# A mixture-of-experts layer on one core: the first chunk's router weights are turned, applied as a bias and split in another order

## What is computed

```
xn = layernorm(x)
x  = x + graph(xn, edges) + attention_and_mlp(xn)
f  = layernorm(x)
w  = softmax(f @ Wr + br)                     # router, 8 weights a row
h  = relu(bn1(f @ W1[e] + b1[e]))             # for each expert e
h  = relu(bn2(h @ W2[e] + b2[e]))
x  = x + sum_e w[:, e] * (h @ Wo[e] + bo[e])
```

## Time and profile before

| | |
|---|---|
| device time, median of 3 runs | 1095.93 us (1095.89 to 1095.94) |
| profiled execution, device time | 1095.72 us |
| its span | 1093.9 us |
| PE busy | 1082.8 us, 99% of the span |
| DVE busy | 768.1 us, 70% |
| ACT busy | 732.0 us, 67% |
| POOL busy | 248.3 us, 23% |
| mean granted TensorE clock | 0.998 |
| chunk 0's expert rounds | about 176 to 219 us of the span |

### The profile page before, as it was taken

How to read it: one execution, slowest core, us unless ns; L and a number is a source line. 1 busy time by engine, 2 the same in 40 slices (tenths; PEclk the granted TensorE clock), 3 DMA queues, 4 the chain that set the end, 5 groups by cost and what they waited for, 6 DMA issues and landing times.

```text
span 1093.9 us, 19080 instructions
## 1 busy us (share of the span) xinstructions
PE 1082.8 (99%) x6512; PEld 967.6 (88%) x6512; DVE 768.1 (70%) x1804; ACT 732.0 (67%) x1275; POOL 248.3 (23%) x290
## 2 busy tenths in 40 slices
PE   9999998999999999999999999999999999999998
PEld 7988987988888888888898888888888988889998
DVE  8888756886686676766766767767767667676665
ACT  5777756676675666756756767667567566576665
POOL 4787763312012012030120120210301202100000
PEclk9999999999999999999999999999999999999999
DMA  6878852111011101110110111101101101100000
GB/s 182 270 226 252 243 171 54 60 34 55 1 49 50 40 18 42 40 58 2 44 55 1 49 50 39 47 13 40 59 1 49 50 10 35 35 20 1 1 20 15
DMA packets 71300, 67.91 MB, mean 62 GB/s; under 512 B 20641, under 2 KB 66579, under 8 KB 71203
## 3 DMA queue, kind: packets, MB, share of 16 engines
q1 hardware_dynamic: 66552, 59.34, 18.1%
q0 software_dynamic: 3968, 6.71, 2.4%
q10 hardware_dynamic: 683, 0.64, 0.2%
HBM read 40.87 MB, written 25.80 MB: 61 GB/s over the span
## 4 chain that ended last, share of the span: by engine, by line
PE 91%; POOL 3%; DVE 2%; issue 2%; ACT 1%; DVEq 0%; POOLq 0%; ACTq 0%
PE bank L280 29%; PE bank L281 29%; PE bank L282 29%; PE bank L989 1%; POOL gathered L601 1%; PE bank L1156 1%; PE bank L1164 1%; PE bank L930 1%; PE bank L1179 1%; PE bank L922 1%; POOL gathered L619 0%; POOL alpha_l L621 0%; PE bank L946 0%; DVE sum_squares L1336 0%; DVE activated L1260 0%
## 5 line engine op out<-in xcount | busy, mean ns | idle before, releaser
L1380 DVE SCALAR_TENSOR_TENSOR accumulated<-bank,router_w,accumulated 128x256 f32<-128x256 f32 (+2 forms) x392 | 170.4, 480 | 177.9 <-PE bank L282 171.0
L665 ACT ACTIVATE h<-weight_stage 128x512 fp32r<-128x512 f32 (+2 forms) x206 | 113.6, 599 | 183.9 <-PE bank L282 164.4
L282 PE MATMUL bank<-ffn_w_high,h 128*128 128x256 f32 (+2 forms) x778 | 220.0, 283 | 0.0
L281 PE MATMUL bank<-ffn_w_low,h 128*128 128x256 f32 (+2 forms) x778 | 219.8, 283 | 0.0
L280 PE MATMUL bank<-ffn_w_high,h 128*128 128x256 f32 (+2 forms) x778 | 219.6, 282 | 0.0
L1230 DVE TENSOR_TENSOR h_low<-activated,h_high 128x512 fp32r<-128x512 f32 (+2 forms) x208 | 135.3, 658 | 76.0 <-ACT h_high L665 73.0
L816 ACT ACTIVATE activated<-bank,bn_cols 128x512 f32<-128x512 f32 (+2 forms) x208 | 155.8, 749 | 46.1 <-PE bank L282 44.1
L816 ACT ACTIVATE weight_stage<-bank,bn_cols 128x512 f32<-128x512 f32 (+2 forms) x208 | 152.7, 748 | 41.4 <-PE bank L282 41.0
L280 PE MATMUL bank<-xT_high,ffn_w_high 128*128 128x512 f32 (+2 forms) x416 | 158.9, 382 | 0.1
L280 PE MATMUL bank<-h_high,ffn_w_high 128*128 128x512 f32 (+2 forms) x416 | 157.9, 380 | 0.1
L281 PE MATMUL bank<-xT_low,ffn_w_high 128*128 128x512 f32 (+2 forms) x416 | 157.8, 379 | 0.0
(11 more groups left out here) (228 smaller groups left out, 1917.1 us busy)
## 6 DMA issues: line engine op xcount, KB each, us to landing
x_rows<-in_x SPq DMA_DIRECT2D x18, 512.0 KB, 4.8
x_turned<-xT_high SPq DMA_DIRECT2D x22, 256.0 KB, 3.6
x_turned<-xT_low SPq DMA_DIRECT2D x22, 256.0 KB, 4.7
out<-accumulated SPq DMA_DIRECT2D x11, 512.0 KB, 3.3
mix_xT_high<-x_turned SPq DMA_DIRECT2D x10, 512.0 KB
mix_xT_low<-x_turned SPq DMA_DIRECT2D x10, 512.0 KB
weight_stage<-in_L_ffn_W SPq DMA_DIRECT2D x16, 256.0 KB, 3.2
node_table<-gathered SPq DMA_DIRECT2D x22, 132.0 KB, 2.9
```

Of the source, the lines that this page charges most:

```text
L281: nc.tensor.matmul(dst, ah, bl, start=False, stop=False)
L282: last = nc.tensor.matmul(dst, al, bh, start=False, stop=(k == n - 1))
L665: return nc.scalar.activation(dst, src, ACT.Copy)
L1380: last = V.scalar_tensor_tensor(a, y_of(ch, e)[b][0:tp, (t % 2) * D:(t % 2 + 1) * D], wts(ch)[0:tp, t, e:e + 1], a, ALU.mult, ALU.add)
```

## The change

All of it concerns chunk 0. PE turns the router weights behind `L2` of round 1 in place of round 0, and multiplies them with `bo` behind `L2` of round 2 in place of round 1. ACT copies the turned weights at the end of `relu2(1)` in place of `relu2(0)`. DVE does `hid1(1)` ahead of `weights` in place of behind them, does `add_bias` in round 2, behind `hid1(3)`, in place of round 1, and `accumulate(0)` no longer waits for `add_bias`; `accumulate(1)` and later do. No instruction with work in it is added or removed; only order and waits are changed.

```diff
@@ ACT
                     relu2(ch, e)
-                    if e == 0 and ch.c == 0:
+                    if e == 1 and ch.c == 0:
                         router_turned(ch)
@@ PE
                     L2(ch, e)
                     if ch.c == 0:
-                        if e == 0:
+                        if e == 1:
                             router_turn(ch)
-                        elif e == 1:
+                        elif e == 2:
                             out_bias(ch)
@@ DVE, accumulate
-                need(dve, s["fai"], ch.b0 + ch.nb)
+                need(dve, s["fai"], ch.b0 + ch.nb if ch.c > 0 else min(e, 1))
@@ DVE, add_bias
                     need(dve, s["fbo"], ch.b0 + b + 1)
+                    if ch.c == 0:
+                        need(dve, s["acc"], 1)
@@ DVE, ahead of the loop and in it
             hid1(CHUNKS[0], 0)
             route(CHUNKS[0])
+            hid1(CHUNKS[0], 1)
             weights(CHUNKS[0])
...
-                    if e + 1 < NE:
+                    if ch.c == 0 and e == 0:
+                        pass
+                    elif e + 1 < NE:
                         hid1(ch, e + 1)
...
-                    if e == 1 and ch.c == 0:
+                    if e == 2 and ch.c == 0:
                         add_bias(ch)
                     if e > 0:
                         accumulate(ch, e - 1)
```

## The result

| | before | changed |
|---|---|---|
| median, beside each other (13 runs each) | 1095.88 us | 1098.41 us |
| ratio, 95% interval | | 1.0025 [1.0017, 1.0034] |
| span of the profiled execution | 1093.9 us | 1096.3 us |

The account below looks back on a forecast made before the run. PE, busy 99% of the span, was taken as the bound. The profiled 1095.72 + 1.63 (later `mix2`) + 1.6 (clock) = 1098.95; for the median, 1095.93 + 3.2 = 1099.1 us, range 1097.1 to 1099.9.

Parts of the forecast that it names:

- first two cases: `mix2`'s new wait with a slow stretch behind it, 1099.1 +- 0.4, chance 0.65; wait alone, 1097.6 +- 0.3, chance 0.21.
- signs of being wrong: `logits` starting before 187.0, DVE's chain from 188.8 to 194.5 being shorter, or the clock staying at 1.00.
- The change at its own place: Chunk 0: `L1(2)` starts at 181.62, held by ACT; moving `hid1(1)` brings nothing; `router_turn` waits for nothing; PE 2.4 us ahead.
- The first place where the gain goes: DVE's `logits` of chunk 1 stays at 187.35; `L2(2)` waits 1.1 us for `hid1(2)`; PE's lead shrinks to 0.93 us.
- The second place: `mix2` of chunk 1 waits 2.5 us for the later `add_bias` and starts at 194.56.
- 1.63 us later than before: `mix2` of chunk 1 starts at 194.56 in place of 192.93.
- the old place costs 1.6 + 1.6 us: At `router_turn`, chunk 0: wait 1.6 us plus slow stretch 1.6 us, 3.2 us, the most the change could bring.
- The clock, 1.6 us: Behind `mix2`'s new wait: a stretch at clock 0.50, priced between 0 and 1.6 us, taken as 1.6.
- The lower bound: Clock price of 0: a wait of 1.5 us ahead of 174.50 left the clock at 1.00.
- the second case: `mix2`'s new wait alone, with the clock left at full: 1097.6 +- 0.3 us, chance 0.21.

Follow-up runs that it names:

- weights_first: The changed kernel with `weights` ahead of `hid1(1)` on DVE again, as before: 1098.08 us beside 1095.73, ratio 1.0025.
- bias_late_alone: The kernel before with only `add_bias` of chunk 0 moved to round 2 behind `hid1(3)`, with its waits: 1099.85 us, ratio 1.0033.
- exp_behind: The changed kernel with `add_bias` ahead of `weigh`, `hid1(2)` ahead of `logits`, and `router_exp` behind `relu1(1)`: 1092.25 us beside 1095.54, ratio 0.9973.
- after_look: The changed kernel itself, profiled a second time; no timed ratio; from the first transposition, `mix2` starts at 20.88 us and the span ends at 923.4.

## Why the prediction was right, and where it was off

The direction was right, and 1098.41 lies in the range, 0.7 us below the predicted 1099.1. The mechanism, `mix2` waiting for a late `add_bias`, was right too. But the time was hit partly by luck: it lies between the prediction's first two cases (1098.7 to 1099.5 and 1097.3 to 1097.9) and in neither. One of its own signs of being wrong, a clock that stays at 1.00, came in the first profile.

- *The change at its own place*: right. `L1(2)` waits 0.84 us for ACT, `router_turn` for nothing, and in the first profile the slow stretch is gone. Moving `hid1(1)` brought nothing (weights_first).
- *The first place where the gain goes*: right. `logits` stays, at 12.9 for 13.0, and `L2(2)` waits: `L1(3)` started at 187.26, took 1.35, and `L2(2)` started at 189.61, so 1.0 us from start to start (1.1 forecast); the profile shows 0.84, since the last matmul's modelled end lies behind its slot.
- *The second place*: right to 0.1 us. 194.56 - 174.32 = 20.24 was forecast, 20.18 measured (PE started 0.15 us behind `add_bias`, not 0.05), and bias_late_alone shows that this part alone does it.
- *The term "1.63 us later than before"*: mis-sized. It was taken against a profile of before with a slow stretch. Against one without it, it is 20.18 - 17.90 = 2.3 us, and the ends agree: 921.1 - 918.8 = 2.3. Behind this is the sentence that the old place costs 1.6 + 1.6 us, the most that the change could bring. The slow stretch costs 0.7 there and not 1.6, because `logits` holds DVE and DVE holds PE. I had found this limit for the changed kernel and hadn't asked it of the kernel before. And exp_behind gained 3.3 us by the medians with a later `router_turn` in it, if not by that alone.
- *The clock, 1.6 us*: right in kind, wrong as a fixed term. The stretch is there in the profiles of after_look and of bias_late_alone, where it cost its 1.5 to 1.6 us, and not in the first profile of the changed kernel or in that of weights_first, which have the same wait of 2.11 us; 6 of the 13 timed runs had a mean clock of 1.000. The lower bound doesn't hold as a rule either: the wait of 1.5 us ahead of the transposition, which had left the clock at 1.00, was followed by half clock 1.7 us later in after_look. So the length of the wait, on which the choice of 1.6 rested, doesn't decide it. By the chances of the prediction, the profiled run is the second case, at 1097.6, which was too low by the 0.7 us of the point above.

The errors offset each other: 1.63 + 1.6 = 3.2 forecast, 2.3 and some share of 1.6 found. Runs of both kernels with equal mean clock differ by 1098.33 - 1095.62 = 2.7 us at 1.000, and by 1098.80 - 1096.12 = 2.7 at 0.998. The profiles give 2.3; the other 0.4 is within the interval of the ratio, and I can't place it. The runs of before in this subtraction were not taken beside those of the changed kernel; with those of the later comparisons at 1.000 (1095.27) it gives 3.1, so it isn't good to 0.4 us.

## What to carry to other kernels

When a step is moved to fill a wait, list who waits for its semaphores downstream: here `mix2` waited for a bank to be read, which no data dependence of the moved sum would show. Look at what the moved instruction stands behind on its own engine; `add_bias`, 0.69 us of work, ended 5 us later. And before a wait or a slow stretch is priced at its length, work out what holds the engine next without it, in the kernel before as much as in the changed one.

## What the runs showed of the hardware

- The same wait of 1.59 us on PE was followed by 3.4 us of granted clock 0.50 in one profile of the same kernel and by full clock in the next, and in bias_late_alone. A wait of 2.1 us gave both too (the two profiles of the changed kernel). One of 2.7 us, seen once, was followed by the half clock; in one of 3.8 us, seen once, it began 2.5 us into the wait and lasted 6.8. The Trainium skill, TensorE: Matmul & The Clock Gate, section "HAM oscillation — how this bites in real kernels", speaks of longer waits only; the falls behind the waits of 1.59, 2.1 and 2.7 us disagree with it.
- Half clock with no wait right ahead of it came too: at 9.9 to 13.3 us in three profiles, with PE busy from 1.12 us on. The first transposition was then at 176.65 to 176.71 us, for 173.90 to 175.15 in the others, so it shifts the whole kernel by about 2 us. It would explain the 3 of 28 runs of before at 1097.44 to 1097.70 us, where the others took 1094.61 to 1096.23; the profiles don't show these runs.
